# Row sums of a recurrence step: squares first and in two halves, the scale row moved, the scaled product in one piece

## The reference, cut to what matters

```
sa    = einsum('bhij,bhj->bhi', state, -kk_t)
state = w_t[..., None]*state + sa[..., None]*(kk_t*a_t)[:, :, None, :] + k_t[..., None]*v_t[:, :, None, :]
norm  = sqrt(mean(state*state, axis=-1, keepdims=True))
state = state / (norm + 1e-5)
o_t   = sum(state * r_t[..., None], axis=-1)
```

## Time and profile before

| what | value |
|---|---|
| median of three runs | 2405.66 us (2405.3 to 2405.74) |
| the profiled execution's own time | 2399.92 us |
| its span, first to last instruction | 2398.1 us |
| VectorE busy | 2143.1 us, 89% of the span |
| ScalarE / TensorE / GpSimd busy | 1652.0 / 1859.0 / 957.3 us |
| granted TensorE clock, mean | 0.823 |

### The profile page before, as it was taken

How to read it: one execution, slowest core, us unless ns; L and a number is a source line. 1 busy time by engine, 2 the same in 40 slices (tenths; PEclk the granted TensorE clock), 3 DMA queues, 4 the chain that set the end, 5 groups by cost and what they waited for, 6 DMA issues and landing times.

```text
span 2398.1 us, 48519 instructions
## 1 busy us (share of the span) xinstructions
PE 1859.0 (78%) x12321; PEld 1508.5 (63%) x12321; DVE 2143.1 (89%) x8462; ACT 1652.0 (69%) x5481; POOL 957.3 (40%) x1608
## 2 busy tenths in 40 slices
PE   5888888788888878877878788778887877343887
PEld 3555555455677767767767777677776767343554
DVE  5888887689709999999999999999999999999887
ACT  4888888577656666666777777777676666555776
POOL 0000000011106565556555666555666555666110
PEclk7999999799988787878788777887777776666999
DMA  5000000000000000000000000000000000000011
GB/s 186 18 18 22 18 22 13 13 1 1 1 1 1 1 1 1 1 1 1 1 1 1 1 1 1 1 1 1 1 1 1 1 1 1 1 1 1 4 33 36
DMA packets 14358, 25.06 MB, mean 10 GB/s; under 512 B 1280, under 2 KB 12032, under 8 KB 13824
## 3 DMA queue, kind: packets, MB, share of 16 engines
q1 hardware_dynamic: 14080, 21.97, 3.1%
HBM read 12.27 MB, written 4.19 MB: 7 GB/s over the span
## 4 chain that ended last, share of the span: by engine, by line
DVE 54%; issue 22%; PE 13%; ACT 5%; POOL 0%; DVEq 0%; POOLq 0%; ACTq 0%
DVE bank L1596 9%; DVE bank L1588 9%; DVE U L1627 8%; DVE pn L1577 7%; DVE xs L1572 5%; DVE kv L1619 4%; PE bank L282 3%; PE bank L267 3%; ACT prob L923 2%; DVE bank L1616 2%; PE bank L585 2%; DVE small L1610 1%; DVE bank L1603 1%; PE bank L669 1%; PE bank L632 1%
## 5 line engine op out<-in xcount | busy, mean ns | idle before, releaser
L750 PE MATMUL bank<-U,ident 128*128 128x128 f32 x2048 | 463.8, 398 | 149.3 <-ACT go L1064 132.5
L1778 POOL TENSOR_TENSOR wu<-U,stg 128x256 f32<-128x256 f32 x512 | 318.1, 621 | 596.5 <-DVE U L1627 596.5
L750 PEld LDWEIGHTS bank<-U,ident 128*128 128x128 f32 x2048 | 429.7, 255 | 187.6 <-issue 156.4
L761 PE MATMUL bank<-stack,tm 128*128 128x64 f32 x1792 | 292.9, 339 | 119.3 <-ACT tm L994 109.7
L1254 ACT ACTIVATE xs<-U 128x128 f32<-128x128 f32 x1024 | 261.5, 301 | 177.8 <-DVE U L1627 173.5
L1577 DVE TENSOR_REDUCE pn<-xs 128x16 f32<-128x256 f32 x1024 | 379.1, 411 | 3.7 <-issue 1.1
L761 PEld LDWEIGHTS bank<-stack,tm 128*128 128x128 f32 x1792 | 282.2, 251 | 136.9 <-ACT tm L994 125.3
L1707 POOL TENSOR_TENSOR kv<-stg 128x256 f32<-128x256 f32 x513 | 317.9, 620 | 0.0
L1572 DVE TENSOR_TENSOR xs<-U,bank 128x128 f32<-128x128 f32 x1024 | 244.6, 280 | 63.9 <-ACT bank L1107 62.6
L1596 DVE TENSOR_TENSOR bank<-wu,bank 128x128 f32<-128x128 f32 x1024 | 293.5, 287 | 1.9 <-POOL wu L1778 1.7
L735 PE MATMUL bank<-wcat,yT 128*128 128x224 f32 x1024 | 288.2, 439 | 6.2 <-issue 5.8
(11 more groups left out here) (213 smaller groups left out, 3589.6 us busy)
## 6 DMA issues: line engine op xcount, KB each, us to landing
out_x<-x SPq DMA_DIRECT2D x8, 512.0 KB, 2.9
x<-in_x SPq DMA_DIRECT2D x1, 3584.0 KB, 16.6
Vs<-V SPq DMA_DIRECT2D x8, 384.0 KB, 4.6
Vs<-V SPq DMA_DIRECT2D x8, 288.0 KB, 3.3
lane<-in_lanes SPq DMA_DIRECT2D x8, 256.0 KB, 3.2
wcat<-in_wcat SPq DMA_DIRECT2D x1, 1792.0 KB, 14.5
wraw<-in_w_up SPq DMA_DIRECT2D x1, 1024.0 KB, 18.7
wraw<-in_w_down SPq DMA_DIRECT2D x1, 1024.0 KB, 11.4
```

The costliest lines, as they stand in the source:

```text
L750: last = pe.matmul(rsum.rearrange("p (t i) -> p t i", i=HD), ident[:, :], steps[:, :, :, j], start=(j == 0), stop=(j == HD - 1))
L761: last = pe.matmul(bank[3 + g][:, e * CH:(e + 1) * CH], tm[:, g * (PB // 2) + e, :, :].rearrange("p a c -> p (a c)"), stack[:, :], start=T ...
L1778: pool.tensor_tensor(ij(wu[:, :]), ij(U[:, half if j else 1 - half, (j - 1) % STEPS, :]), col(stg[:, half, j, TW, :]), ALU.mult).then_inc( ...
```

## The change

1. The row sum over 256 numbers per half becomes two over 128: `square_sums` (both halves of the squares) right behind x0 and x1, then the sums of the products. Four instructions where there were two. The sums of squares count a semaphore of their own (`ps`), and ScalarE's `root` waits for that alone.
2. The scale row moves from between d0 and d1 to ahead of d0, right behind the outer products z0 and z1.
3. In three of four steps the scaled product `kv` is one instruction over 256 numbers and stands between d0 and d1. In the fourth, the reciprocal stands between d0 and d1; the two products stay in halves.
4. `add_output(n, m, 1)` stands behind d1. The sums after the last step use the same helper.

```diff
--- before.py
+++ after.py
@@ -214,8 +214,8 @@
         C = {n: sem("c_" + n) for n in (
             "bs mc ag ve rs nm tz yn yt yc hal yd cv x1 pj ev tr rc").split()}
         S = {n: sem("s_" + n) for n in (
-            "ln rt sg lam kk ka wu k0 rsum rse").split()}
-        T = [{n: sem(f"t{e}_" + n) for n in "u x sq pn z d k".split()} for e in range(2)]
+            "ln rt sg lam kk ka k ps wu k0 rsum rse").split()}
+        T = [{n: sem(f"t{e}_" + n) for n in "u x sq pn z d".split()} for e in range(2)]
         G = {n: sem("g_" + n) for n in "kv e1 wd e2 wc ka g1 gm g2 f1 ls f2 fc".split()}
         O = {n: sem("o_" + n) for n in "ov os t1 t1c gs gt gc pr sq ln sd dn rs t x".split()}
         Z = {n: sem("z_" + n) for n in "rs os t1 goa god gt gc pr sq rt dn iv".split()}
@@ -1151,8 +1151,7 @@
 
             def root(t1):
 
-                for e in range(2):
-                    act.wait_ge(T[e]["pn"], t1)
+                act.wait_ge(S["ps"], 2 * t1)
                 act.activation(lnr.rearrange("p (e i) -> p e i", e=2), pn[:, :, 1, :], ACT.Ln, scale=1.0 / HD).then_inc(S["ln"], 1)
                 act.wait_ge(S["ln"], t1)
                 act.activation(rt, lnr, ACT.Exp, scale=0.5).then_inc(S["rt"], 1)
@@ -1555,6 +1554,16 @@
                     dve.wait_ge(O["dn"], i + 1)
                     dve.reciprocal(oss[:, 2, 0:1], oss[:, 2, 0:1]).then_inc(O["rs"], 1)
 
+            def square_sums(t):
+
+                for e in range(2):
+                    dve.wait_ge(T[e]["sq"], t)
+                    dve.tensor_reduce(pn[:, e, 1, :], ij(xs[:, e, 1, :]), AXX, ALU.add).then_inc(S["ps"], 1)
+
+            def difference(e, t1):
+                dve.wait_ge(T[e]["z"], t1)
+                dve.tensor_tensor(rows8(zz, e), rows8(wu, e), rows8(zz, e), ALU.subtract).then_inc(T[e]["d"], 1)
+
             for n in range(NCH):
                 for pair in range(NB // 2):
                     for half in range(2):
@@ -1571,12 +1580,10 @@
                                 dve.wait_ge(T[e]["u"], t0 + j)
                                 dve.tensor_tensor(ij(xs[:, e, 0, :]), ij(rows8(U[:, half if j else 1 - half, (j - 1) % STEPS, :], e)),
                                                   row(kkr[:, jj, :], i=HD // 2), ALU.mult).then_inc(T[e]["x"], 1)
+                            square_sums(t0 + j)
                             for e in range(2):
                                 dve.wait_ge(T[e]["x"], t1)
-                                dve.wait_ge(T[e]["sq"], t0 + j)
-                                dve.tensor_reduce(pn[:, e, :, :].rearrange("p a i -> p (a i)"),
-                                                  xs[:, e, :, :].rearrange("p a (i j) -> p (a i) j", j=HD), AXX,
-                                                  ALU.add).then_inc(T[e]["pn"], 1)
+                                dve.tensor_reduce(pn[:, e, 0, :], ij(xs[:, e, 0, :]), AXX, ALU.add).then_inc(T[e]["pn"], 1)
                             if jj == 1:
                                 dve.wait_ge(G["ls"], it * 2 + (g + 1))
                             if jj == 2:
@@ -1589,47 +1596,41 @@
                                                   row(kkar[:, g, jj, :], i=HD // 2), ALU.mult).then_inc(T[e]["z"], 1)
                             if j == 6:
                                 add_output(n, m, 0)
-                            for e in range(2):
-                                dve.wait_ge(T[e]["z"], t1)
-                                if e == 0:
-                                    dve.wait_ge(S["wu"], t1)
-                                dve.tensor_tensor(rows8(zz, e), rows8(wu, e), rows8(zz, e), ALU.subtract).then_inc(T[e]["d"], 1)
-                                if e == 1:
-                                    continue
-                                dve.wait_ge(S["rt"], t1)
-                                if jj == 0:
-                                    dve.tensor_scalar(sring[:, 3, :], rt, LN_EPS, None, ALU.add).then_inc(S["sg"], 1)
-                                else:
-                                    dve.scalar_tensor_tensor(sring[:, jj - 1, :], sring[:, (jj + 2) % RENORM, :], LN_EPS, rt,
-                                                             ALU.mult, ALU.add).then_inc(S["sg"], 1)
+                            dve.wait_ge(S["rt"], t1)
+                            if jj == 0:
+                                dve.tensor_scalar(sring[:, 3, :], rt, LN_EPS, None, ALU.add).then_inc(S["sg"], 1)
+                            else:
+                                dve.scalar_tensor_tensor(sring[:, jj - 1, :], sring[:, (jj + 2) % RENORM, :], LN_EPS, rt,
+                                                         ALU.mult, ALU.add).then_inc(S["sg"], 1)
+                            dve.wait_ge(S["wu"], t1)
+                            difference(0, t1)
+                            dve.wait_ge(S["sg"], t1)
+                            if jj == RENORM - 1:
+                                dve.reciprocal(lam, sring[:, jj - 1, :]).then_inc(S["lam"], 1)
+                                difference(1, t1)
+                                dve.wait_ge(S["lam"], it * 2 + (g + 1))
+                                dve.wait_ge(S["k0"], t1)
+                                for e in range(2):
+                                    dve.wait_ge(T[e]["d"], t1)
+                                    dve.tensor_tensor(ij(rows8(zz, e)), ij(rows8(zz, e)), col(lam[:, 8 * e:8 * e + 8], HD // 2),
+                                                      ALU.mult).then_inc(S["k"], 1)
+                            else:
+                                dve.wait_ge(S["k0"], t1)
+                                dve.tensor_tensor(ij(kv), col(sring[:, (jj + 3) % RENORM, :]),
+                                                  ij(kv0[:, j % 2, :]), ALU.mult).then_inc(S["k"], 1)
+                                difference(1, t1)
                             if j == 6:
                                 add_output(n, m, 1)
-                            dve.wait_ge(S["sg"], t1)
-                            if jj == RENORM - 1:
-
-                                dve.reciprocal(lam, sring[:, jj - 1, :]).then_inc(S["lam"], 1)
-                                dve.wait_ge(S["lam"], it * 2 + (g + 1))
-                            dve.wait_ge(S["k0"], t1)
-                            for e in range(2):
-                                if jj == RENORM - 1:
-                                    dve.wait_ge(T[e]["d"], t1)
-                                    dve.tensor_tensor(ij(rows8(zz, e)), ij(rows8(zz, e)), col(lam[:, 8 * e:8 * e + 8], HD // 2),
-                                                      ALU.mult).then_inc(T[e]["k"], 1)
-                                else:
-                                    dve.tensor_tensor(ij(rows8(kv, e)), col(sring[:, (jj + 3) % RENORM, 8 * e:8 * e + 8], HD // 2),
-                                                      ij(rows8(kv0[:, j % 2, :], e)), ALU.mult).then_inc(T[e]["k"], 1)
                             new = kv0[:, j % 2, :] if jj == RENORM - 1 else kv
                             if j == 0:
                                 dve.wait_ge(S["rsum"], it)
                             for e in range(2):
                                 dve.wait_ge(T[e]["d"], t1)
-                                dve.wait_ge(T[e]["k"], t1)
+                                dve.wait_ge(S["k"], t1 + it * 2 + g + (1 if jj == RENORM - 1 and e == 1 else 0))
                                 dve.tensor_tensor(rows8(U[:, half, j, :], e), rows8(zz, e), rows8(new, e),
                                                   ALU.add).then_inc(T[e]["u"], 1)
             dve.wait_ge(S["rt"], L)
-            for e in range(2):
-                dve.wait_ge(T[e]["sq"], L)
-                dve.tensor_reduce(pn[:, e, 1, :], ij(xs[:, e, 1, :]), AXX, ALU.add).then_inc(T[e]["pn"], 1)
+            square_sums(L)
             dve.wait_ge(O["ov"], L // STEPS)
 
             def last_row_sums(t):
```

More of the change, by code:

```diff
@@ L1591, in _ @@
                                 add_output(n, m, 0)
-                            for e in range(2):
-                                dve.wait_ge(T[e]["z"], t1)
-                                if e == 0:
-                                    dve.wait_ge(S["wu"], t1)
-                                dve.tensor_tensor(rows8(zz, e), rows8(wu, e), rows8(zz, e), ALU.subtract).then_inc(T[e]["d"], 1)
-                                if e == 1:
-                                    continue
-                                dve.wait_ge(S["rt"], t1)
-                                if jj == 0:
-                                    dve.tensor_scalar(sring[:, 3, :], rt, LN_EPS, None, ALU.add).then_inc(S["sg"], 1)
-                                else:
-                                    dve.scalar_tensor_tensor(sring[:, jj - 1, :], sring[:, (jj + 2) % RENORM, :], LN_EPS, rt,
-                                                             ALU.mult, ALU.add).then_inc(S["sg"], 1)
-                            if j == 6:
```

(17 more changed lines are left out.)

## The result

The changed kernel takes 2366.7 us (median of four runs, 2362.9 to 2368.1) against 2405.5 for the kernel before. The ratio is 0.9848, with a 95% interval of 0.9832 to 0.9863: 36.5 us or 1.5% faster.

The account below looks back on a forecast made before the run. VectorE's queue bounds the recurrence loop, priced by start distances. Plain steps -4, fourth steps -8, late squares -6 and output norm +1.5 sum to -16.5 us: 2389 us, range 2378 to 2402.

Parts of the forecast that it names:

- The wait of 0.08: Scale row in the recurrence loop: it waits 0.08 us a step for ScalarE's root, hidden under d0's length; claimed to go.
- The product's price: Whole scaled product over 256 numbers in plain steps: start distance 0.33 us, taken from L1344, with L386's 0.39 as upper bound.
- the reciprocal's distance to d1: Every fourth step: d1 starts 0.165 us behind the reciprocal; lower bound 0.07, upper bound 0.285.
- (a): Rival: the whole product costs what L386 costs, 0.06 us more in 384 plain steps, +23 us, 2412; chance 0.05.
- (b): Rival: a new wait before U0 or behind the second sum of squares, 0.02 to 0.03 a step, 2397 to 2404; chance 0.12.
- (d): Rival: the scale row still waits because Ln starts no earlier, 0.08 in 512 steps, +41 us, 2430; chance 0.02.
- Rival (c): Reciprocal releases d1 soon and rare long steps shrink with the slack: 2375 to 2379 us; chance 0.09.
- Rival (e): Fixed costs add in full, each instruction counting with its length: +96 us, 2500; chance 0.01.
- the plain step: Loop steps without the reciprocal, 384 of them: 2.78 us against 2.79, -0.01 each, -4 us.
- the fourth step: Steps with the reciprocal, 128 of them: -0.19 us and +0.13 for the sums, -0.065 each, -8 us (-18 to +6).
- late squares: Step j = 5, 64 times: ScalarE's evacuations delay the squares; the earlier root removes 0.09 us each, -6 us.
- output norm: In 24 steps L1553 and L1556 no longer use VectorE's wait of 0.08 and cost some 0.06 us more, +1.5 us.

## What the prediction had right, and which terms of its sum failed

**The bound and the mechanisms held.** The loop is VectorE's queue, and what counts is start distances. The wait of 0.08 was for the root: with the sums changed it is gone, with the squares last it is back at 0.22, and with the scale row moved alone it shows as idle time. The product's price was that of L1344, 0.33, and the reciprocal's distance to d1 was 0.17 (forecast 0.165). U0 doesn't wait. Rivals (a), (b) and (d) fell. Rival (c) names the time that came nearest (2375 to 2379), but not its reason: the reciprocal released d1 after 0.17 and not after 0.07. Its other half, shorter long steps, is worth 3.4 us at most, the last row but one of the table below.

Rival (e) fell too. Splitting two reduces into four cost 0.12 a step, 0.06 for each further instruction, where fixed costs in full would have asked for 0.30. The Trainium skill ("VectorE: DVE Perf Modes", section on the trn2 errata) has the latency exposed between instructions. The rival read that as the full length of each instruction; the start distances of this case show 0.06 of it, and the measurement decides. The section's formula for the duration of an fp32 tensor_tensor, an estimate of 290 ns for 128 numbers, fits the 0.28 of the traces within 4%.

**What failed is the size of two terms of the sum: the plain step at -0.01, which measured -0.03, and the fourth step at -0.065, which measured -0.12.** Together they hold 15 of the 19.3 us by which the loop gained more than forecast. By median steps:

| steps | before, us | after, us | difference | in the loop | forecast |
|---|---|---|---|---|---|
| plain, j = 0, 1, 2, 4, 6 (320) | 2.80 to 2.84 | 2.77 to 2.80 | -0.031 to -0.038 | -10.9 | -3 |
| plain with late squares, j = 5 (64) | 2.895 | 2.769 | -0.126 | -8.1 | -7 |
| fourth, j = 3, 7 (128) | 3.120 | 3.001 | -0.119 | -15.1 | -8 |
| output norm, mean over the median of j = 6 (24) | +0.072 | +0.142 | +0.070 | +1.7 | +1.5 |
| all else above the medians (long steps) | | | | -3.4 | 0 |
| sum | | | | -35.8 | -16.5 |

- *Plain step, forecast 2.78 against 2.79.* It came out at 2.77 against 2.80. The 2.79 was one step, read from two starts; the median over the loop was 2.80. Of its pieces d0 to scale row was read as 0.27, and the median is 0.28. So the stretch that the scale row and the product stand in gave 0.155, not 0.14. The four sums cost 0.775, not the 0.79 that I priced from the two sums after the last step, 0.20 apart, of which the first had waited for ScalarE; in the loop such sums start 0.193 apart. Against 0.655 before that is 0.12 and not 0.13. Each error is 0.01 to 0.015, and 0.01 in 384 steps is 4 us, as much as the term itself. They all have the same sign, so they add up.
- *Fourth step, "-0.19, and with the sums +0.13".* It was -0.22 and +0.12, and k1 followed k0 by 0.195 and not by 0.208 as before, where k0 had waited for the reciprocal just ahead of it (medians of the start distances). Of the 0.22, 0.02 is d1 to k0, which took 0.182 and not 0.20. The run with the reciprocal moved back shows the place to be worth 18 to 19 us alone.
- *Late squares, 0.09.* One step was taken for all, though the forecast knew of larger ones. The median gain over that of a plain step was 0.09, and by means over the 64 steps it was 0.12: 2 of the 3.4 us in the last row but one of the table. Before, the first sum started over 0.42 behind x0 in 53 of the 64 steps, after the change in none.
- *The list of waits.* The forecast says that past the start d0 is the only line of the loop in it. It is not: the scale row stands there too, `DVE bank L1603 <- ACT small L1158: 1.0, 4, 0.3` and once at L1601 with 0.3. That is 1.3 us of a wait that took 0.08 in each step, some 41 us.
- *Median of runs.* The profiled execution before was 5.7 us below its median, that of after 1.3 above. The stretch behind the loop is the same in both profiles within 0.5 us, and the loop starts 3.5 us later after the change than before (first starts of the loop's line), so the 31.8 us between the two spans understate the loop's 35.8. Of the 22.4 us between forecast and measured median, 19.3 are the loop's terms and 3 come from setting medians against single profiles.

**The parts don't add up.** Alone, in the kernel before, they cost +5, +94 and +44 us. Together they gain 36. The early root is paid for by extra instructions (+5). It makes the scale row's move free, and that move opens two gaps, behind the scale row and behind the reciprocal, for d0 and d1 to stand in (18 us), and a place where the whole product has d1 ahead of its reader (20 us).

## What to carry to other kernels

On an engine that is busy all the time, read start distances and look for one that is longer than the same instruction gives elsewhere: a wait shorter than the instruction ahead of it leaves no idle time, and the list of waits here had 1.3 of some 41 us of it. Where a step repeats hundreds of times, take each distance as a median over the loop, to the nanosecond, before subtracting two sums of fourteen terms; and give the range an error of 0.01 us a step. Look at the steps away from the median as well: one more copy on ScalarE was free by the median and cost 0.07 us in every fourth step of its kind. Merging two instructions paid here only where something independent stood between the merged one and its reader, and the same independent instruction hides the latency of a small one such as a scale or a reciprocal.

## What the runs showed that I had not expected

The scattered long steps are not noise. Against the median of their j, 71 steps of the changed kernel are over 0.04 us too long, and together all steps carry 13.7 us. In the second run of the same kernel they are the same 71 steps, and no step differs by more than 0.006 us from its twin. One of them, step 270 counted from 0, at U and the next x0:

```profile
1494.61 0.48 DVE L1630 TENSOR_TENSOR U<-bank,kv 128x128 f32<-128x128 f32 x2
1495.09 0.48 DVE L1581 TENSOR_TENSOR xs<-U,bank 128x128 f32<-128x128 f32 x2
```

From U0 to x0 it takes 0.48, and 0.49 in the second run, where 0.40 is usual.

The 71 are of three kinds. Twenty-four are the steps with the output norm, 3.4 us, whose cause is known. One is the first step, 1.5 us. The other 46 carry 8.8 us, and they follow a count. Number VectorE's instructions in the trace, semaphore instructions too: each of the 46 steps contains one of the places that lie 128 instructions apart (within one instruction), though only 17% of all steps do.

The programs bear it out. Beside output norm and first step, the kernel with the scale row moved back has 42 long steps; it has as many VectorE instructions as the changed kernel, 12301, and all 42 are among the 46. The changed kernel with the product in halves has 36 and 12685 instructions, as the kernel before: it shares 2 with the changed kernel and 23 with the kernel before. With the reciprocal moved back there are 12429 instructions and 41 long steps, which share 3 with the one and 7 with the other. So the long steps go with the count of instructions in front of them and not with the execution. What VectorE does at these places no run shows.

The spread between runs comes from elsewhere: over the profiles here the loop starts between 714 and 727 us, while the length of the one loop that was profiled twice repeats within 0.1 us. For a change inside the loop, its first and last start thus tell about 1 us where the medians of runs tell 5.
